# Routed experts without a token get no tile, and all expert weights are loaded ahead of the routed loop

## The chip, the cores and the metric

The kernel runs on one core of one Trainium2 chip. The metric is the device time of one execution in microseconds (us), with the inputs in HBM and the output written back to HBM. Shorter is better.

## The reference

Four sequences of 256 tokens of 256 float32 channels (1,024 tokens in all) pass a gated additive attention term and then a gated mixture of experts:

```python
si = einsum('bnd,d->bn', ctx, Wi[0]);  sj = einsum('bnd,d->bn', ctx, Wj[0])
xij = sigmoid(si[:, :, None] + sj[:, None, :] + b[0])
x = x + tanh(g_xattn[0]) * (0.6 * xij + 0.4 * layernorm(x))

xf = layernorm(x).reshape(-1, 256)                  # 1024 tokens
scores = sigmoid(xf @ w_router)                     # 32 experts
sfc = scores + corr_bias
grp = sfc.reshape(T, 8, 4)                          # 8 groups of 4
group_scores = top_k(grp, 2)[0].sum(-1)             # the best 4 groups stay
topk_idx = top_k(where(score_mask, sfc, -inf), 6)   # 6 experts a token
combine = zeros((T, 32)).at[...].add(take_along_axis(scores, topk_idx))
g = einsum('th,ehm->etm', xf, gate_w); u = einsum('th,ehm->etm', xf, up_w)   # M = 176
eo = einsum('etm,emh->eth', silu(g) * u, down_w)
routed = einsum('te,eth->th', combine, eo)
shared = silu(xf @ sh_gate_w) * (xf @ sh_up_w) @ sh_down_w                   # M = 352
x = x + tanh(g_ffn[0]) * (routed + shared)
```

There are 1,024 x 6 = 6,144 pairs of token and expert. How they fall on the experts depends on the inputs.

## The kernel before

The kernel is written engine by engine, with semaphores by hand. All is float32.

**Ahead of the routed loop.** The sequencer of SyncE (SP) starts the loads of the inputs, the shared weights and then the expert weights, four experts in four transfers (`load_expert_weights`, L215: gate, up, and two parts of down). Before the loop it does so for the first 20 of 32 transfers (`FIRST`, L56, L247), that is for the first 20 experts. In the meantime the engines work out the attention term, both layer norms, the router and the choice of experts, and after that the shared expert in 16 units.

**Sorting.** Every expert owns a region of 1,152 rows in a DRAM buffer, `rows_dram`. A row has 289 numbers (1,156 bytes): 256 channels, 32 combine weights and the token's number. GpSimd scatters the rows of the 1,024 tokens there, six copies each, in 48 indirect transfers of 128 rows (L365). Behind an expert's last row 128 pad rows are written, so that its last tile is full: for 20 experts by SP (L253 to L256), for 12 (`ACT_PADS`) by ScalarE's queue (L467 to L471). One more block of 128 pads, the idle one, stands behind all regions (L251). GpSimd's queue also clears two buffers for the sums (L359).

**The table of tiles.** VectorE turns the counts of rows into numbers of tiles of 128 rows each, at least one for every expert (L901 to L903), and from that makes a table with the expert and the first row of every tile. The numbers of rounds come from the total: `last` is one plus how many of 11, 15, 19, ... are below the total (L906 to L908, L336), and 4 x last + 7 tiles are run (`RING` is 4, `REST` is 3). Surplus tiles read the idle block.

**The routed loop.** For each tile SP loads 128 rows (L272; the first load waits for all pads and all scatters, L266 and L267). PE transposes x (L649), multiplies with gate and up (L578), transposes h (L584, L585) and multiplies with down (L593, L594). ScalarE copies, applies silu and scales; VectorE copies and gates; GpSimd adds the result to one of the two sums in DRAM by an indirect accumulating transfer (L384). Tiles run in rounds of four, with four buffers for the rows. In SP's first rounds (`LATE`, L57) a reload of each buffer is followed by one of the 12 late weight transfers (L284 to L287). The rounds after that stand in a loop with an If on `last` (L288). PE waits for the first 20 transfers before its first tile (L656) and for the other 12 after four rounds (L698). At the end SP loads the two sums, VectorE adds them and SP stores the output.

Of the kernel before, what the change touches and what calls it, by code (L numbers as in the profile page):

```python
# [18 lines left out]
ALU = mybir.AluOpType  # L19
ACT = mybir.ActivationFunctionType  # L20

P = 128
# [5 lines left out]
RING = 4  # L28
# [5 lines left out]
def gated_xattn_moe(nc, x, ctx, g_xattn, g_ffn, w_adj, b_adj, w_router, corr_bias, gate_w, up_w, down_w,  # L34
# [3 lines left out]
    E, _, M = gate_w.shape  # L38
# [7 lines left out]
    PAIRS = T * TOPK  # L46
    TILES = (PAIRS - E) // P + E
    FULL, REST = TILES // RING, TILES % RING
# [4 lines left out]

    PLACED = [range(0, GROUP), range(GROUP, 2 * GROUP), range(2 * GROUP, J)]
    SUMS = 2
    FIRST = E * 5 // 8  # L56
    LATE = 1 + (E - FIRST) // RING  # L57
    PAD_TURN = 7
    ACT_PADS = 12
    TABLE_TURN = 6  # L60
# [2 lines left out]
    with ExitStack() as stack:  # L63
# [6 lines left out]
        def sem(name):  # L70
            return stack.enter_context(nc.semaphore(name))
# [53 lines left out]
        cnt_i = sb("cnt_i", [P, 2, E], I32)  # L125
        ntile = sb("ntile", [P, E])
# [6 lines left out]
        tile_of = sb("tile_of", [P, 2])  # L133
        used = sb("used", [P, 1])
        tiles = sb("tiles", [2, P], I32)
        LEAST = -(-(E - REST) // RING) - 1
        round_ends = sb("round_ends", [1, FULL - 2])
        round_ends_i = sb("round_ends_i", [1, FULL - 2], I32)
        round_is = sb("round_is", [1, FULL - 2])
# [39 lines left out]

        s_xin = [sem(f"s_xin{b}") for b in range(B)]  # L180
        s_ctx, s_wadj, s_gates, s_cb, s_wr = (sem(n) for n in ("s_ctx", "s_wadj", "s_gates", "s_cb", "s_wr"))
        s_shw, s_expw = sem("s_shw"), [sem("s_expw0"), sem("s_expw1")]

        s_const, s_clear = sem("s_const"), sem("s_clear")

# [29 lines left out]
        def load_expert_weights(eng, n):  # L215

            e = n // 4 * 4
            if n % 4 < 2:  # L220
                w, cols = ((gate_w, slice(0, M)), (up_w, slice(M, 2 * M)))[n % 4]
                ins = eng.dma_start(wgu[:, e:e + 4, :, cols].rearrange("p e k m -> p (e k) m"),  # L222
                                    w[e:e + 4].rearrange("e (k p) m -> p (e k) m", p=P))
            elif n % 4 == 2:
                ins = eng.dma_start(wd0[:, e:e + 4, :], down_w[e:e + 4, 0:P, :].rearrange("e p c -> p e c"))  # L225
            else:
                ins = eng.dma_start(wd1[:, e:e + 4, :], down_w[e:e + 4, P:M, :].rearrange("e p c -> p e c"))  # L227
            ins.then_inc(s_expw[0 if e < FIRST else 1], 16)

        @block.sync  # L230
        def _(sp):
# [9 lines left out]
            for s in range(SH):  # L241
# [2 lines left out]
                sp.dma_start(sgu[:, s, :, M:2 * M], sh_up_w[:, cols].rearrange("(k p) m -> p k m", p=P)).then_inc(s_shw, 16)  # L244
                sp.dma_start(sd0[:, s, :], sh_down_w[s * M:s * M + P, :]).then_inc(s_shw, 16)
                sp.dma_start(sd1[:, s, :], sh_down_w[s * M + P:(s + 1) * M, :]).then_inc(s_shw, 16)
            for n in range(FIRST):  # L247
                load_expert_weights(sp, n)

            sp.wait_ge(s_const, 4)  # L250
# [23 lines left out]
            def reload(i, s):  # L274
                t = i * RING + s

                sp.wait_ge(s_xT, t - (RING - 1))
                sp.wait_ge(s_taken, t - (RING - 1))
                load(t, s)

            load(0, 0, first_row)
            for s in range(1, RING):
                load(s, s)
            for i in range(1, LATE):  # L284
                for s in range(RING):
                    reload(i, s)
                    load_expert_weights(sp, FIRST + (i - 1) * RING + s)  # L287
            with sp.Fori(LATE, FULL) as i:  # L288
                with sp.If(i < last + 1):
                    for s in range(RING):  # L290
                        reload(i, s)
# [226 lines left out]
        def _(pe):  # L518
# [3 lines left out]
            for j in range(J):  # L522
                ins = nc.tensor.transpose(pX[j // 4][0:D, (j % 4) * P:(j % 4 + 1) * P], ctx_sb[:, j, :], ident[:, :])
# [129 lines left out]
                pe.wait_ge(s_xTc, t + 1)  # L653
                gate_up(None, par, lambda k: xT[:, par, k, :], lambda k: wgu[:, bass.ds(e, 1), k, :])

            pe.wait_ge(s_expw[0], 16 * FIRST)  # L656

            def look_up(t):
                return pe.value_load(tiles[0:1, bass.ds(t, 1)], min_val=0, max_val=E - 1)
# [9 lines left out]
            def iteration(i, first=False, tiles=None):  # L669


                e = e_next = None
                for s in range(tiles or RING):
                    left = tiles - s if tiles else RING
                    t = i * RING + s
                    e_before, e = e, e_next
                    if left > 2:
                        transpose_x((s + 2) % RING, i + (s + 2) // RING + 1, s % 2)
                    if left > 1:
                        e_next = look_up(t + 1)  # L680
                        routed_gate_up(t + 1, (s + 1) % 2, e_next)

                    if s == 0 and not first:
                        e_before = look_up(t - 1)
                    if s == 1:
                        e_before = look_up(t - 1)
                    turn_h(t + UNITS, s % 2)
                    if e_before is not None:
                        routed_down(t - 1, (s + 1) % 2, e_before)
                return e  # L690

            early = (FIRST - 1) // RING
            iteration(0, first=True)
            with pe.Fori(1, early) as i:
                iteration(i)
            pe.wait_ge(s_expw[1], 16 * (E - FIRST))  # L698
            last = load_last(pe)
            with pe.Fori(early, FULL - 1) as i:  # L700
                with pe.If(i < last):
                    iteration(i)
            e_last = iteration(last, tiles=RING + REST)
# [5 lines left out]
        def _(dve):  # L709
# [3 lines left out]
            def link(ins):  # L713

                made[0] += 1
                ins.then_inc(s_dve, 1)
                dve.wait_ge(s_dve, made[0])
# [182 lines left out]

            link(V.tensor_scalar(cnt_i[:, 0, :], ntile[:, :], float(P - 1), None, ALU.add))  # L901
            link(V.tensor_scalar(cnt_i[:, 1, :], cnt_i[:, 0, :], P.bit_length() - 1, None, ALU.logical_shift_right))
            link(V.tensor_scalar(ntile[:, :], cnt_i[:, 1, :], 1.0, None, ALU.max))  # L903
            link(V.tensor_tensor_scan(tend[:, :], ntile[:, :], zero_e[:, :], 0.0, ALU.add, ALU.add))

            link(V.tensor_scalar(round_is[:, :], round_ends[:, :], tend[0:1, E - 1:E], None, ALU.is_lt))  # L906
# [97 lines left out]
```

## Time and profile before

| | us |
|---|---|
| median of 3 runs | 329.17 |
| lowest and highest | 328.31, 332.16 |
| span of the profiled execution | 334.7 |

| engine | busy us | share of the span |
|---|---|---|
| PE (matmul) | 274.3 | 82% |
| PE (weight load) | 160.8 | 48% |
| DVE | 126.2 | 38% |
| ACT | 99.2 | 30% |
| POOL | 166.9 | 50% |

The profile is one execution, recorded by the hardware profiler; its span is 5.5 us above the median of the runs that were only timed. Engines: PE is TensorE, DVE VectorE, ACT ScalarE, POOL GpSimd, SP SyncE; SPq is SP's sequencer, which issues transfers. Busy shares are means over stages with different limits. The DMA share is the mean busy share of the core's 16 DMA engines; where packets overlap it comes to a little over 1. In all, 57.20 MB are moved. L12 is line 12 of the kernel.

### The profile page before, as it was taken

To read this page: it belongs to the slowest core of one execution; us is meant where nothing else is said; L and a number is where in the kernel's file an instruction comes from. 1 tells how busy PE (TensorE), PEld (TensorE's weight loads), DVE (VectorE), ACT (ScalarE), POOL (GpSimd) and SP (SyncE) were. 2 spreads that over 40 slices of the span, in tenths; PEclk is the share of its full clock that TensorE was granted. 3 is DMA by queue.
4 is the path that set the end of the run, shared out by engine and by line. 5 is a ranking of instruction groups with operands and counts; after the bars stand their busy time and mean duration, and the time that the engine had idled before them with its cause. 6 is when DMAs were issued, how large, how long until landed. Compare 5 with 4: busy or idle time off the path is not lost.

```text
span 334.7 us, 6384 instructions
## 1 busy us (share of the span) xinstructions
PE 274.3 (82%) x1107; PEld 160.8 (48%) x1108; DVE 126.2 (38%) x627; ACT 99.2 (30%) x267; POOL 166.9 (50%) x145
## 2 busy tenths in 40 slices
PE   4673879999205997998999999999999999999700
PEld 3531445555002654655565655555566555665300
DVE  4568689433100331332333333333333333333214
ACT  3452411111001332333333333333333333333200
POOL 3334777777700153344555555555555555465620
PEclk9999999999655998999999999999999999999955
DMA  5899999999974589995666566666666666664577
GB/s 157 266 319 366 352 343 314 314 230 254 240 154 114 156 211 259 229 249 91 100 99 99 98 100 89 113 100 89 96 109 96 94 100 100 100 99 71 59 170 240
DMA packets 58557, 57.20 MB, mean 171 GB/s; under 512 B 6544, under 2 KB 56432, under 8 KB 58544
## 3 DMA queue, kind: packets, MB, share of 16 engines
q1 hardware_dynamic: 43520, 36.51, 39.6%
q0 software_dynamic: 13136, 18.78, 34.0%
q10 hardware_dynamic: 1888, 1.78, 2.5%
q8 instruction: 4, 0.07, 0.1%
q14 instruction: 9, 0.07, 0.1%
HBM read 32.35 MB, written 24.70 MB: 170 GB/s over the span
## 4 chain that ended last, share of the span: by engine, by line
PE 53%; SPq 24%; DMA 15%; issue 4%; DVE 1%; ACT 1%; DVEq 0%; POOLq 0%; ACTq 0%
PE pG L578 23%; PE pY L594 11%; PE pY L593 8%; PE pX L649 7%; DMA sum_dram<-xnT,idx 6%; SPq L225 5%; SPq L222 5%; DMA rows_dram<-pad_rows 4%; SPq L227 4%; SPq L255 4%; DMA rows<-rows_dram 3%; SPq L256 3%; PE pH L584 2%; PE pH L585 2%; DMA xnT<-sum_dram 1%
## 5 line engine op out<-in xcount | busy, mean ns | idle before, releaser
L384 POOL DMA_INDIRECT sum_dram<-xnT,idx x71 | 110.0, 1549 | 119.1 <-ACT xnT L486 94.9
L578 PE MATMUL pG<-wgu,rows 128*128 x284 | 99.9, 476 | 2.0 <-ACT rows L476 1.5
L855 DVE COPY hT<-pH 128x128 f32<-128x128 f32 x87 | 25.3, 291 | 119.7 <-PE pH L585 117.9
L578 PEld LDWEIGHTS pG<-wgu,rows 128*128 128x128 f32 x284 | 49.9, 196 | 19.8 <-issue 5.4
L365 POOL DMA_INDIRECT rows_dram<-rows,row_i x48 | 47.3, 986 | 21.3 <-issue 14.2
L486 ACT ACTIVATE xnT<-pY,wt 128x256 f32<-128x256 f32 x71 | 33.7, 474 | 73.9 <-PE pY L594 41.8
L462 ACT ACTIVATE sg<-pG 128x176 f32<-128x176 f32 x87 | 27.6, 317 | 90.9 <-PE pG L578 90.9
L594 PE MATMUL pY<-wd,hT 48*128 x142 | 49.4, 428 | 0.0
L649 PE MATMUL pX<-ident,rows 128*128 128x128 f32 x142 | 31.7, 306 | 21.0 <-DMA rows<-rows_dram 21.0
L593 PE MATMUL pY<-wd,hT 128*128 x142 | 42.6, 382 | 0.0
L649 PEld LDWEIGHTS pX<-ident,rows 128*128 128x128 f32 x142 | 14.8, 144 | 44.8 <-issue 40.1
L476 ACT ACTIVATE rows<-pX 128x256 f32<-128x256 f32 x71 | 26.9, 379 | 27.7 <-PE pX L649 25.4
L594 PEld LDWEIGHTS pY<-wd,hT 48*128 48x128 f32 x142 | 20.9, 184 | 23.5 <-issue 23.5
L851 DVE TENSOR_TENSOR h<-sg,pG 128x176 f32<-128x176 f32 x87 | 27.8, 319 | 4.9 <-ACT sg L462 4.9
L939 DVE COPY wt<-rows 128x1 f32 x71 | 10.9, 154 | 38.2 <-issue 20.4
L584 PE MATMUL pH<-ident,h 128*128 128x128 f32 x87 | 24.1, 277 | 0.9 <-DVE h L851 0.9
L585 PE MATMUL pH<-ident,h 128*48 128x128 f32 x87 | 23.9, 274 | 0.0
L856 DVE COPY hT<-pH 48x128 f32<-48x128 f32 x87 | 23.7, 273 | 0.0
L578 PE MATMUL pG<-sgu,xnT 128*128 128x352 f32 x64 | 22.9, 481 | 0.0
L593 PEld LDWEIGHTS pY<-wd,hT 128*128 128x128 f32 x142 | 21.6, 193 | 0.8 <-issue 0.3
L584 PEld LDWEIGHTS pH<-ident,h 128*128 128x128 f32 x87 | 12.3, 142 | 12.1 <-DVE h L851 2.9
L943 DVE COPY idx<-rows 128x1 int32<-128x1 int32 x71 | 10.6, 149 | 12.4 <-DMA sum_dram<-xnT,idx 12.2
(145 smaller groups left out, 168.7 us busy)
## 6 DMA issues: line engine op xcount, KB each, us to landing
rows<-rows_dram SPq DMA_DIRECT2D x71, 144.5 KB, 2.2
wgu<-in_L_ffn_gate_w_dram SPq DMA_DIRECT2D x8, 704.0 KB, 7.6
wgu<-in_L_ffn_up_w_dram SPq DMA_DIRECT2D x8, 704.0 KB, 9.1
wd<-in_L_ffn_down_w_dram SPq DMA_DIRECT2D x8, 512.0 KB, 8.4
rows_dram<-pad_rows SPq DMA_DIRECT2D x21, 144.5 KB, 12.7
sum_dram<-pad_rows POOLq DMA_DIRECT2D x2, 1152.0 KB, 10.9
rows_dram<-pad_rows ACTq DMA_DIRECT2D x12, 144.5 KB, 8.4
wd<-in_L_ffn_down_w_dram SPq DMA_DIRECT2D x8, 192.0 KB, 7.4
```

The source lines that it names most:

```text
L365: pool.indirect_dma_start(rows_dram[:, :], bass.IndirectOffsetOnAxis(ap=row_i[:, j, k:k + 1], axis=0), rows[:, j, :], None).then_inc(s_sca ...
L384: pool.indirect_dma_start(sums_dram[s % SUMS][:, :], bass.IndirectOffsetOnAxis(ap=idx[:, s:s + 1], axis=0), y[:, s, :], None, compute_op=A ...
L462: nc.scalar.activation(sg[:, par, :], pG[par][:, 0:M], ACT.Silu).then_inc(s_silu, 1)
L476: nc.scalar.activation(xT[:, par, :, :].rearrange("p k t -> p (k t)"), pX[par][:, 0:K * P], ACT.Copy).then_inc(s_xTc, 1)
L486: nc.scalar.activation(y[:, s, :], pY[s % 2][:, 0:H], ACT.Copy, scale=wt[:, s:s + 1]).then_inc(s_yc, 1)
L578: ins = nc.tensor.matmul(pG[par][:, 0:2 * M], left(k), w(k), start=(k == 0), stop=(k == K - 1))
L584: nc.tensor.transpose(pH[par][:, 0:P], h[:, par, 0:P], ident[:, :])
L585: nc.tensor.transpose(pH[par][0:M2, P:2 * P], h[:, par, P:M], ident[:, :]).then_inc(s_hT, 1)
L593: nc.tensor.matmul(bank[:, 0:H], hT[:, par, 0, :], w0, start=start, stop=False)
L594: ins = nc.tensor.matmul(bank[:, 0:H], hT[0:M2, par, 1, :], w1, start=False, stop=stop)
L649: ins = nc.tensor.transpose(pX[par][:, k * P:(k + 1) * P], xg[:, s, k * P:(k + 1) * P], ident[:, :])
L851: V.tensor_tensor(h[:, par, :], sg[:, par, :], pG[par][:, M:2 * M], ALU.mult).then_inc(s_h, 1)
```

## The change

Three things change. The number of tiles of an expert is no longer raised to one where it has no rows. All 32 weight transfers are issued by SP ahead of its pads, under one semaphore, and the loop's reloads stand in one loop with an If. PE waits for all weights before the first tile, and its rounds stand in one loop with an If from round 1 on. `LEAST`, a lower bound that is declared for the value of `last`, follows the new least number of tiles.

```diff
--- before.py
+++ after.py
@@ -53,8 +53,6 @@
 
     PLACED = [range(0, GROUP), range(GROUP, 2 * GROUP), range(2 * GROUP, J)]
     SUMS = 2
-    FIRST = E * 5 // 8
-    LATE = 1 + (E - FIRST) // RING
     PAD_TURN = 7
     ACT_PADS = 12
     TABLE_TURN = 6
@@ -133,7 +131,7 @@
         tile_of = sb("tile_of", [P, 2])
         used = sb("used", [P, 1])
         tiles = sb("tiles", [2, P], I32)
-        LEAST = -(-(E - REST) // RING) - 1
+        LEAST = -(-(PAIRS // P - REST) // RING) - 1
         round_ends = sb("round_ends", [1, FULL - 2])
         round_ends_i = sb("round_ends_i", [1, FULL - 2], I32)
         round_is = sb("round_is", [1, FULL - 2])
@@ -179,7 +177,7 @@
 
         s_xin = [sem(f"s_xin{b}") for b in range(B)]
         s_ctx, s_wadj, s_gates, s_cb, s_wr = (sem(n) for n in ("s_ctx", "s_wadj", "s_gates", "s_cb", "s_wr"))
-        s_shw, s_expw = sem("s_shw"), [sem("s_expw0"), sem("s_expw1")]
+        s_shw, s_expw = sem("s_shw"), sem("s_expw")
 
         s_const, s_clear = sem("s_const"), sem("s_clear")
 
@@ -225,7 +223,7 @@
                 ins = eng.dma_start(wd0[:, e:e + 4, :], down_w[e:e + 4, 0:P, :].rearrange("e p c -> p e c"))
             else:
                 ins = eng.dma_start(wd1[:, e:e + 4, :], down_w[e:e + 4, P:M, :].rearrange("e p c -> p e c"))
-            ins.then_inc(s_expw[0 if e < FIRST else 1], 16)
+            ins.then_inc(s_expw, 16)
 
         @block.sync
         def _(sp):
@@ -244,7 +242,7 @@
                 sp.dma_start(sgu[:, s, :, M:2 * M], sh_up_w[:, cols].rearrange("(k p) m -> p k m", p=P)).then_inc(s_shw, 16)
                 sp.dma_start(sd0[:, s, :], sh_down_w[s * M:s * M + P, :]).then_inc(s_shw, 16)
                 sp.dma_start(sd1[:, s, :], sh_down_w[s * M + P:(s + 1) * M, :]).then_inc(s_shw, 16)
-            for n in range(FIRST):
+            for n in range(E):
                 load_expert_weights(sp, n)
 
             sp.wait_ge(s_const, 4)
@@ -281,11 +279,7 @@
             load(0, 0, first_row)
             for s in range(1, RING):
                 load(s, s)
-            for i in range(1, LATE):
-                for s in range(RING):
-                    reload(i, s)
-                    load_expert_weights(sp, FIRST + (i - 1) * RING + s)
-            with sp.Fori(LATE, FULL) as i:
+            with sp.Fori(1, FULL) as i:
                 with sp.If(i < last + 1):
                     for s in range(RING):
                         reload(i, s)
@@ -653,7 +647,7 @@
                 pe.wait_ge(s_xTc, t + 1)
                 gate_up(None, par, lambda k: xT[:, par, k, :], lambda k: wgu[:, bass.ds(e, 1), k, :])
 
-            pe.wait_ge(s_expw[0], 16 * FIRST)
+            pe.wait_ge(s_expw, 16 * E)
 
             def look_up(t):
                 return pe.value_load(tiles[0:1, bass.ds(t, 1)], min_val=0, max_val=E - 1)
@@ -691,13 +685,9 @@
 
 
 
-            early = (FIRST - 1) // RING
             iteration(0, first=True)
-            with pe.Fori(1, early) as i:
-                iteration(i)
-            pe.wait_ge(s_expw[1], 16 * (E - FIRST))
             last = load_last(pe)
-            with pe.Fori(early, FULL - 1) as i:
+            with pe.Fori(1, FULL - 1) as i:
                 with pe.If(i < last):
                     iteration(i)
             e_last = iteration(last, tiles=RING + REST)
@@ -900,7 +890,7 @@
 
             link(V.tensor_scalar(cnt_i[:, 0, :], ntile[:, :], float(P - 1), None, ALU.add))
             link(V.tensor_scalar(cnt_i[:, 1, :], cnt_i[:, 0, :], P.bit_length() - 1, None, ALU.logical_shift_right))
-            link(V.tensor_scalar(ntile[:, :], cnt_i[:, 1, :], 1.0, None, ALU.max))
+            link(V.tensor_copy(ntile[:, :], cnt_i[:, 1, :]))
             link(V.tensor_tensor_scan(tend[:, :], ntile[:, :], zero_e[:, :], 0.0, ALU.add, ALU.add))
 
             link(V.tensor_scalar(round_is[:, :], round_ends[:, :], tend[0:1, E - 1:E], None, ALU.is_lt))
```

## Rows read from the trace of the kernel before

**Rows 1.** The page, PE and DMA in 40 slices of the span, tenths.
```profile
PE   4673879999205997998999999999999999999700
...
DMA  5899999999974589995666566666666666664577
```

**Rows 2.** Windows by stage: length, busy by engine, granted clock, DMA share, GB/s.
```profile
12.00:20.00 8.00, 4.41 (x13) 2.25 (x11) 5.54 (x18) 5.05 (x12) 2.40 (x3) 1.00 1.07 321
28.00:58.00 30.00, 23.40 (x99) 12.66 (x100) 24.14 (x141) 6.24 (x16) 22.82 (x24) 1.00 1.09 338
58.00:66.00 8.00, 7.72 (x31) 4.33 (x30) 3.87 (x18) 0.95 (x3) 6.17 (x7) 1.00 1.07 328
66.00:98.00 32.00, 19.45 (x73) 10.75 (x72) 7.40 (x28) 1.91 (x6) 19.77 (x21) 0.82 1.05 230
98.00:102.00 4.00, 0.00 (x0) 0.00 (x0) 0.00 (x0) 0.00 (x0) 0.00 (x0) 0.50 0.15 47
...
160.00:300.00 140.00, 140.00 (x594) 83.66 (x595) 47.92 (x249) 54.07 (x149) 76.52 (x50) 1.00 0.63 99
```

**Rows 3.** Timeline of SP's queue: start us, us, line, transfer, count.
```profile
11.14 0.43 SPq L222 DMA_DIRECT2D wgu<-in_L_ffn_gate_w_dram  x1
...
16.72 0.45 SPq L222 DMA_DIRECT2D wgu<-in_L_ffn_gate_w_dram  x1
...
58.24 0.47 SPq L251 DMA_DIRECT2D rows_dram<-pad_rows  x1
60.33 27.93 SPq L256 DMA_DIRECT2D rows_dram<-pad_rows  x20
101.38 4.88 SPq L272 DMA_DIRECT2D rows<-rows_dram  x5
```

**Rows 4.** Waits of SP's queue, 85 to 105 us: total, times, longest.
```profile
SPq L267 <- DMA rows_dram<-rows,row_i: 9.4, 1, 9.4
SPq L272 <- DMA rows_dram<-pad_rows: 1.8, 1, 1.8
```

**Rows 5.** Chain of waits, the piece before the first load: start us, us, what.
```profile
87.66 13.55 DMA rows_dram<-pad_rows
```

**Rows 6.** Timeline of POOL, the last of its 48 scatters.
```profile
90.90 0.96 POOL L365 DMA_INDIRECT rows_dram<-rows,row_i  x1 [0.30 <-issue]
```

**Rows 7.** Timeline of PE, first transpose of h of tiles 1, 13 and 68.
```profile
112.35 0.27 PE L584 MATMUL pH<-ident,h 128*128 128x128 f32 x1
...
153.44 0.27 PE L584 MATMUL pH<-ident,h 128*128 128x128 f32 x1
...
309.27 0.27 PE L584 MATMUL pH<-ident,h 128*128 128x128 f32 x1
```

**Rows 8.** The page's DMA issues: count, KB each, median us to landing.
```profile
rows<-rows_dram SPq DMA_DIRECT2D x71, 144.5 KB, 2.2
wgu<-in_L_ffn_gate_w_dram SPq DMA_DIRECT2D x8, 704.0 KB, 7.6
wgu<-in_L_ffn_up_w_dram SPq DMA_DIRECT2D x8, 704.0 KB, 9.1
wd<-in_L_ffn_down_w_dram SPq DMA_DIRECT2D x8, 512.0 KB, 8.4
rows_dram<-pad_rows SPq DMA_DIRECT2D x21, 144.5 KB, 12.7
...
wd<-in_L_ffn_down_w_dram SPq DMA_DIRECT2D x8, 192.0 KB, 7.4
```

**Rows 9.** DMA queue q1 (SP's), packets, MB, share: 66 to 98, 329.8 to 334.6 us.
```profile
q1 hardware_dynamic: 2382, 2.45, 36.8%
...
q1 hardware_dynamic: 1110, 1.07, 66.3%
```

## The prediction

> **What bounds the kernel now.** I read the 40 slices of the page first. The reader is to see two stages with different limits. In the first, up to about 98 us, the DMA row stands at 8 and 9 while PE comes and goes, and PE is empty just before the routed loop; in the second, PE stands at 9 until the last two slices and DMA at about 6 [rows 1]. The windows by stage put numbers on that: DMA share 1.05 to 1.09 in every stretch from 12 to 98 us, then 0.63 with PE busy 140.00 of 140 us [rows 2].
>
> Next come SyncE's own queue and the chain of waits. SP issues five groups of four experts' weights from 11.14 on. It spends 58.24 - 16.72 = 41.5 us on the last four, 10.4 us each. At 58.24 it reaches the pads: one, then twenty that take it 27.9 us, and the first routed load goes out at 101.38 [rows 3]. SP waits for the scatters 9.4 us and for pads 1.8 us before that load [rows 4], and the chain runs back through a pad of 13.55 us [rows 5]. So pads and scatters end together, and what ends them is the volume that 16 busy DMA engines must move. GpSimd issued its last scatter at 90.90 [rows 6]. The routed loop itself is bound by PE.
>
> PE's first transpose of h in each tile is a good clock for the loop. From 153.44 to 309.27 it ticks 55 times in 155.83 us, 2.833 us a tile. From 112.35 (tile 1) to 153.44 (tile 13) it needs 41.09 us where 12 tiles at that pace are 34.0, so 7.1 us are lost while the last twelve weight transfers run beside the loop. From 309.27 (tile 68) to the span's end are 25.4 us [rows 7].
>
> **Removed: tiles.** The kernel runs whole rounds of four tiles after the first seven, 4 x last + 7. Working out the reference's routing on its own inputs gives 7 of 32 experts without a token and 64 tiles by the rounded-up counts, 71 when each absent expert gets one. 71 needs last = 16, thus 71 tiles, which is the count of routed loads on the page [rows 8]. 64 lies over 63, so last = 15 and 67 tiles run: seven tiles go, but only one round. Four tiles by 2.833 are **11.3 us off PE's path**. Clearing or padding does not shrink: the pads still go out for all 32 experts. The replaced VectorE instruction works on the same 32 columns as before and I cost it at nothing: all of it is hidden, since the table is through long before 101 us. The If that now guards rounds 1 to 3 as well is the one that rounds 4 to 15 already carry at an unbroken 2.833, and the rounds skipped at the end (two before, three after) leave no gap at the tail that I can see; nothing for both. Were such a skip to cost as much as 0.5 us, it would show as a gap on PE.
>
> **Moved: three groups of weights.** Each is 704 + 704 + 512 + 192 KB [rows 8], 2.16 MB, together 6.49 MB in twelve transfers, from between the reloads to ahead of the pads on SP's queue. Queued behind them on SP are all 21 of its pads, and behind those the first routed load; PE, ScalarE, VectorE and GpSimd all wait for that load. PE's wait for all weights costs nothing of its own, as they stand ahead of the pads on the same queue.
> - Gain in the loop: SP and the DMA engines are free of weights there. The stage behind it (share 0.63) shows no loss, so I take back **7.1 us**, all of it.
> - Cost ahead of the loop, the disputed term d. I work it out by volume. From 58 to 98 us 2.63 + 7.36 = 10.0 MB move (328 GB/s for 8 us, 230 for 32) and 0.2 MB more in the next 4 [rows 2]. Of these 21 pads of 0.148 MB, 3.1 MB, are SP's. After the change weights, scatters and ScalarE's 12 pads run together: 10.2 - 3.1 + 6.5 = 13.6 MB. The row nearest to that mix is 58 to 66 us, all three kinds at once, at 328 GB/s: 41.4 us, to 99.6. Then SP's 3.1 MB of pads run last. The nearest row for pads is 66 to 98 us at 230 GB/s: 13.5 us, to 113.1. The engines used to fall idle at 98, so **d = 15 us**, and the first load goes out at 101.4 + 15 = 116.4.
> - Bounds of d. Low: the mix at the 338 GB/s of 28 to 58 us [rows 2] is 40.2 us, and lone pads as fast as the stores of the output, 1.07 MB in 66.3% of 4.8 us or 336 GB/s [rows 9], are 9.2 us; end 107.6, d = 9.6. High by volume: the weights simply added at the 321 GB/s that SP's queue made alone from 12 to 20 us [rows 2] are 20.2 us. Higher still is the second rival. I keep 230 for the pads since it is the only row with these 1156-byte rows written.
>
> The Trainium skill, page "DMA: Bandwidth & Descriptors", section "Measured", gives 425 GB/s for one core streaming a large transfer. The three groups would then be an estimated 15.3 us in place of 20.2 when simply added. The traces here show 321 to 338 over any stretch with weights, so I keep the rows.
>
> **The sum.** Tile 1 turns at 112.35 + 15 = 127.35; tile 64, the third last of 67, 63 ticks later at 305.8; 25.4 us on, the span ends at 331.3. Or: 334.7 - 11.3 - 7.1 + 15 = 331.3 us, 3.4 us less. The profiled execution stands at 334.7 where the median of the runs is 329.17; I carry the difference of 3.4 over and predict **325.8 us**, 1.0% less. The break-even is d = 18.4. A measurement of this kernel can tell about 2%, 6.6 us, from no change; that is d below 11.8 or above 25.
>
> **The rivals.**
> - *Likeliest, within 2%* (d from 11.8 to 25), chance 0.65. The gains and the delay nearly cancel, whichever of the two volume counts holds.
> - *Faster by over 2%*, chance 0.24. Two things could bring it. Pads left alone could drain at the 336 GB/s of a lone store queue [rows 9], with reads of weights mixed well with writes of scatters (338 beside scatters against 321 alone, [rows 2]): d = 9.6, end 334.7 - 18.4 + 9.6 = 325.9, median 320.4. Against it: 230 GB/s from 66 to 98 us was all writes of short rows, and dropping ScalarE's and GpSimd's share does not make those rows longer.
> - *Slower by over 2%: the pads keep their pace.* Chance 0.11. SP comes to the pads three groups of 10.4 later, at 89.4, and they then take what they took before: from the first of the twenty at 60.33 to the last one's landing at 101.2 [rows 3, 5], 40.9 us. They start 2.1 later, so 91.5 + 40.9 = 132.4, d = 31, end 347.3, median 341.8. For it: nothing in the trace shows SP's pads by themselves. Against it: they were slow while scatters and ScalarE's pads took their turns, with SP's queue holding 36.8% of the engines' time from 66 to 98 us [rows 9]; GpSimd's scatters end at 90.90 and do not wait for SP. It decides from d = 25, which is pads at 3.1 MB in 23.5 us, 132 GB/s.
>
> The Trainium skill, page "DMA: Bandwidth & Descriptors", section "Queues, rings and completion order", says that each DMA engine takes turns among the queues that have work. By that rule a lone pad queue gets the whole engine, which speaks against this rival; no run here shows it yet.
> - *The tile count doesn't fall as counted.* Chance under 0.02, within the 0.11. If the kernel's own rounding left 68 or more tiles, all 71 would run: 342.6, median 337.1. Expert counts close to a multiple of 128 (639 to 640, 139 to 128) are not near enough to add four.
>
> **How the numbers follow.** The faster case holds 0.24, no change 0.65, slower 0.11. The range that leaves no more than 2 in 10 out takes d from 9.6 less a microsecond, 319.5, to d of about 23, 334; within the likeliest alone it is 322.5 to 335.7.
>
> **What would show it.** SP's first pad at 89 to 97 us. DMA share at or over 1 without a break from 12 to about 110 us, with more than 320 GB/s up to some 99 and 200 to 340 after. The first routed load at 116 (111 to 122); 131 refutes the volume count and shows the slow rival. PE's tiles 2.83 apart from the second on, 67 of them, so that the loop from first load to last tile loses no 7 us. The tail from the third last tile unchanged at 25.4. Wrong would be: a gap on PE in the loop's first rounds (then something other than weights made it), 71 or 63 loads, or pads that land long after the engines' share has fallen below 1.

## The result

The changed kernel takes 342.62 us (median of 4, 342.49 to 343.85), the kernel before 329.18 us. The ratio is 1.0385, with a 95% interval from 1.0331 to 1.0438: slower by 3.9%, where 1.0% faster was forecast. The range ended at 334.0. A later set of runs on another chip gave 1.0382 (1.0302 to 1.0463).

The profiled execution of the changed kernel spans 340.8 us, 6.1 more than the 334.7 of the profile before. That is less than half of the 13.4 us between the medians. The time of an execution is its span plus 1.6 to 2.0 us in every kernel measured since. If that held for the profile before as well, its execution took some 336.5 us, 7 above the median; that time itself is not known.

Page of the changed kernel, PE, granted clock, DMA and GB/s in 40 slices (to set beside [rows 1]):

```profile
PE   3673889999200008999999999999999999999800
...
PEclk9999999999855555999999999999999999999965
DMA  5999999999983332366656665665655656664478
GB/s 154 285 313 355 344 348 353 353 304 314 310 278 107 104 104 69 70 102 98 101 97 98 101 98 96 99 100 93 103 99 98 101 97 97 98 101 72 50 146 268
```

Windows by stage of the same kernel (length, busy by engine, granted clock, DMA share, GB/s; to set beside [rows 2]):

```profile
66.00:98.00 32.00, 21.15 (x80) 11.76 (x79) 7.64 (x29) 2.22 (x7) 19.71 (x21) 0.88 1.08 318
98.00:108.00 10.00, 0.00 (x0) 0.00 (x0) 0.00 (x0) 0.00 (x0) 0.00 (x0) 0.50 0.47 153
...
112.00:116.00 4.00, 0.00 (x0) 0.00 (x0) 0.00 (x0) 0.00 (x0) 0.00 (x0) 0.50 0.32 105
...
120.00:124.00 4.00, 0.00 (x0) 0.00 (x0) 0.00 (x0) 0.00 (x0) 0.00 (x0) 0.50 0.33 110
```

The stage that the forecast did not have stands in the slices: between the busy DMA stage and the loop there are 28 us in which every compute engine is idle while the DMA engines fall to a share of a third, 105 to 117 GB/s in the windows from 108 to 124 us. Bandwidth is not what is short there. Timeline of SP's queue (start us, us, line, transfer, count; to set beside [rows 3]):

```profile
95.00 1.30 SPq L225 DMA_DIRECT2D wd<-in_L_ffn_down_w_dram  x1
96.34 0.44 SPq L249 DMA_DIRECT2D rows_dram<-pad_rows  x1
98.10 26.11 SPq L254 DMA_DIRECT2D rows_dram<-pad_rows  x20
125.94 184.41 SPq L270 DMA_DIRECT2D rows<-rows_dram  x67
```

The last of the weights is issued at 95.00, the twenty pads take SP 26.1 us, and the first load follows at 125.94. Ahead of that load SP's queue waited for pads once, for 0.2 us, and not for scatters (before: 9.4 and 1.8 us for scatters and pads, [rows 4]):

```profile
SPq L270 <- DMA rows_dram<-pad_rows: 0.2, 1, 0.2
```

The chain of waits of the changed kernel shows what one pad is made of (start us, us, what):

```profile
120.67 0.27 SPq L253
121.37 0.33 SPq L254
121.85 0.27 SPq L253
122.67 0.34 SPq L254
123.17 0.27 SPq L253
123.87 1.90 DMA rows_dram<-pad_rows
125.94 0.36 SPq L270
```

L253 is the look-up of the pad's address in a table (0.27 us, up to 0.57 at the start of a group of four) and L254 the issue (0.34 us). With the register arithmetic, the check of the value and the loop's own steps between them, the twenty take 26.11 us, 1.31 us each. The chain goes through SP's instructions and not through transfers; only the last landing, 1.90 us, is on it. In the chain of the kernel before the last pad's landing was 13.55 us [rows 5].

Stage by stage, from PE's first transpose of h of each tile (changed kernel, tiles 1 and 64, the third last of 67):

```profile
136.79 0.27 PE L578 MATMUL pH<-ident,h 128*128 128x128 f32 x1
...
316.01 0.27 PE L578 MATMUL pH<-ident,h 128*128 128x128 f32 x1
```

| stage, us | before, profile of the forecast | changed | difference |
|---|---|---|---|
| up to the first routed load | 101.38 | 125.94 | +24.6 |
| first load to tile 1 | 10.97 | 10.85 | -0.1 |
| tile 1 to the third last tile | 196.92 | 179.22 | -17.7 |
| third last tile to the end | 25.43 | 24.79 | -0.6 |
| span | 334.7 | 340.8 | +6.1 |

### The profile page after: what moved, and what is told of

Read it like the earlier page. It is cut to its first block, busy times and chain, and to the rows that moved or that the text cites. A ratio compares the mean times of both kernels' runs of the same rounds, so it can differ in the third digit from the quotient of the medians.

```text
span 340.8 us, 6147 instructions
## 1 busy us (share of the span) xinstructions
PE 261.6 (77%) x1059; PEld 153.8 (45%) x1060; DVE 122.2 (36%) x607; ACT 94.6 (28%) x255; POOL 160.5 (47%) x141
## 3 DMA queue, kind: packets, MB, share of 16 engines
q1 hardware_dynamic: 42944, 35.92, 36.6%
## 4 chain that ended last, share of the span: by engine, by line
PE 55%; SPq 34%; issue 4%; DMA 4%; DVE 1%; POOL 0%; ACT 0%; DVEq 0%; POOLq 0%
PE pG L572 24%; PE pY L588 12%; SPq L223 11%; SPq L220 11%; PE pY L587 8%; PE pX L643 7%; SPq L225 3%; SPq L253 3%; SPq L254 2%; PE pH L579 2%; PE pH L578 2%; DMA xnT<-sum_dram 1%; DMA sum_dram<-xnT,idx 1%; DVE xs L962 1%; DMA rows<-rows_dram 1%
## 5 line engine op out<-in xcount | busy, mean ns | idle before, releaser
L378 POOL DMA_INDIRECT sum_dram<-xnT,idx x67 | 103.8, 1549 | 132.0 <-ACT xnT L480 127.2
L572 PE MATMUL pG<-wgu,rows 128*128 x268 | 92.8, 469 | 0.8 <-issue 0.8
L643 PE MATMUL pX<-ident,rows 128*128 128x128 f32 x134 | 30.0, 306 | 41.4 <-DMA rows<-rows_dram 41.4
L572 PEld LDWEIGHTS pG<-wgu,rows 128*128 128x128 f32 x268 | 46.7, 195 | 16.5 <-issue 2.7
L480 ACT ACTIVATE xnT<-pY,wt 128x256 f32<-128x256 f32 x67 | 31.8, 474 | 69.6 <-PE pY L588 39.7
L588 PE MATMUL pY<-wd,hT 48*128 x134 | 46.6, 428 | 0.0
L587 PE MATMUL pY<-wd,hT 128*128 x134 | 40.1, 381 | 0.0
L470 ACT ACTIVATE rows<-pX 128x256 f32<-128x256 f32 x67 | 25.4, 379 | 49.0 <-PE pX L643 46.0
L929 DVE COPY wt<-rows 128x1 f32 x67 | 10.3, 154 | 59.7 <-DMA rows<-rows_dram 40.6
L572 PE MATMUL pG<-sgu,xnT 128*128 128x352 f32 x64 | 24.3, 504 | 0.0
L587 PEld LDWEIGHTS pY<-wd,hT 128*128 128x128 f32 x134 | 20.2, 191 | 0.7 <-issue 0.3
L578 PEld LDWEIGHTS pH<-ident,h 128*128 128x128 f32 x83 | 11.7, 141 | 11.3 <-DVE h L841 2.9
L572 PEld LDWEIGHTS pG<-sgu,xnT 128*128 128x128 f32 x64 | 11.4, 199 | 7.4 <-issue 4.1
```

The source lines that it names most:

```text
L378: pool.indirect_dma_start(sums_dram[s % SUMS][:, :], bass.IndirectOffsetOnAxis(ap=idx[:, s:s + 1], axis=0), y[:, s, :], None, compute_op=A ...
L480: nc.scalar.activation(y[:, s, :], pY[s % 2][:, 0:H], ACT.Copy, scale=wt[:, s:s + 1]).then_inc(s_yc, 1)
L572: ins = nc.tensor.matmul(pG[par][:, 0:2 * M], left(k), w(k), start=(k == 0), stop=(k == K - 1))
L578: nc.tensor.transpose(pH[par][:, 0:P], h[:, par, 0:P], ident[:, :])
L587: nc.tensor.matmul(bank[:, 0:H], hT[:, par, 0, :], w0, start=start, stop=False)
L588: ins = nc.tensor.matmul(bank[:, 0:H], hT[0:M2, par, 1, :], w1, start=False, stop=stop)
```

## The experiments

Twelve kernels were run in three sets of four, each set on one chip with the kernel before beside it: 329.6 us on the first, 334.87 on the second, 329.9 on the third. Times of different sets are therefore compared by their ratio to the kernel before. Single places of two traces (SP's arrival at the pads, the first load) differ by 3 to 4 us between executions with the same instructions ahead of them, and by more between chips.

### Set 1: the parts of the change, and the pads on another queue

**The kernel before, profiled once more** (no edit).

> The kernel before, profiled once more. The profiled execution on which the prediction rests spans 334.7 us, 5.5 above the median of its runs, while the changed kernel's spans lie 1.7 us below its times. If the first profile caught a long execution, this one spans about 327.5 us, and the 7 us are missing at one place: either the loop's first 13 tiles run at 2.83 us each (no loss beside the late weights), or the first routed load goes out some 7 us before 101.4. If the two ways of timing only differ, the span is 334 to 335 again.

Measured: 329.86 us, 0.9988 of before (0.9943 to 1.0033). The profiled execution spans 329.6. SP's queue, its waits for the scatters and the pads, and the first transposes of h of tiles 1, 13 and 68:

```profile
60.43 26.80 SPq L256 DMA_DIRECT2D rows_dram<-pad_rows  x20
98.67 4.87 SPq L272 DMA_DIRECT2D rows<-rows_dram  x5
```

```profile
SPq L267 <- DMA rows_dram<-rows,row_i: 8.8, 1, 8.8
...
SPq L272 <- DMA rows_dram<-pad_rows: 0.7, 1, 0.7
```

```profile
109.57 0.27 PE L584 MATMUL pH<-ident,h 128*128 128x128 f32 x1
...
149.63 0.27 PE L584 MATMUL pH<-ident,h 128*128 128x128 f32 x1
...
305.46 0.27 PE L584 MATMUL pH<-ident,h 128*128 128x128 f32 x1
```

Neither of the two places alone holds the difference to the first profile. The first load goes out 2.7 us earlier, the loop's first tiles still lose 6.1 us (149.63 - 109.57 = 40.06 for 12 tiles of 2.833), and the tail is 1.3 us shorter. The loss beside the late weights is real. The execution profiled here took 331.44 us, 1.6 above the median, so this profile too is of a longer execution than most, but less so than the first. It is the better one to set the changed kernel against: first load 27.3 us later, tile 1 to third last tile 16.7 us shorter, tail 0.7 longer. Together that is 11.2 us of span.

**The tile part alone.**

```diff
-            link(V.tensor_scalar(ntile[:, :], cnt_i[:, 1, :], 1.0, None, ALU.max))
+            link(V.tensor_copy(ntile[:, :], cnt_i[:, 1, :]))
```

The declared bound `LEAST` follows, as in the change.

> The kernel before with the tile part of the change alone (the 12 late weight transfers stay in the loop; with these inputs no tile of the first four rounds belongs to an expert past the 20th). Both theories: one round of four tiles less at 2.833 us, so 11.3 us less than before, 317.9 us. If the end of the loop were bound by something other than PE, less than that.

Measured: 319.67 us, 0.9719 (0.9631 to 0.9807), 9.9 us less than before. 67 tiles ran, as counted. The tile part does what it says. The first load stands at 97.68 us, where before_again has 98.67.

**The weight part alone** (the same line, and `LEAST`, put back into the changed kernel).

> The changed kernel with at least one tile per expert again: 71 tiles. Weights ahead alone: 11.3 us above the changed kernel, 353.9 us, 24.7 above before. A first load at 126 as in the changed kernel.

Measured: 349.72 us, 1.0634 (1.0532 to 1.0736), so 20.1 us above before. That is 4 us less than expected; 2.7 of them are in the first load, at 123.19 us here and 125.94 in the changed kernel. The pads took SP the same (26.17 us), but it came to them at 93.28 instead of 96.34, with the same instructions ahead of them; so much differs from one execution to the next. The loss is all in the weight part, and the tile part hides half of it.

**All pads of experts on ScalarE's queue.**

```diff
-    ACT_PADS = 12
+    ACT_PADS = 32
...
-            with sp.Fori(0, (E - ACT_PADS) // 4) as q:
-                for i in range(4):
-                    at = sp.value_load(pad_at[0:1, bass.ds(q * 4 + i, 1)], min_val=0, max_val=IDLE - P)
-                    sp.dma_start(rows_dram[bass.ds(at, P), :], pad_rows[:, :]).then_inc(s_pads, 16)
...
-                for e in range(first, min(first + 2, E)) if n >= PAD_TURN else ():
+                for e in range(first, min(first + 2, E) if n < UNITS - 1 else E) if n >= PAD_TURN else ():
```

> The changed kernel with all 32 experts' pads issued by ScalarE's queue (two in each unit of the shared expert from the eighth on, the other 14 after the last unit), none by SP. Theory A, SP's own pace: the twenty pads cost SP 1.35 us each behind the weights, one after another, while the DMA engines stand at a third; then SP is free at 96 us and the first load goes out when the engines have moved all: 13.6 + 3.1 MB from 58 us on at 330 GB/s, 109 to 112 us, time 326 to 330 us. Theory B, pads are slow at the DMA engines when they are alone or last (107 GB/s measured): ScalarE's last 14 pads, 2.1 MB, come as late as 82 us and drain at 107 GB/s, while weights of SP take their turns; first load not before 118 us, time 334 us or more.

Measured: 330.43 us, 1.0021 (0.9982 to 1.0060), 12 us less than the changed kernel with the same bytes and the same tiles. Windows by stage of this kernel, and its SP queue:

```profile
66.00:98.00 32.00, 21.62 (x82) 11.99 (x80) 8.10 (x30) 2.22 (x7) 20.13 (x21) 0.90 1.10 295
98.00:110.00 12.00, 0.00 (x0) 0.00 (x0) 0.00 (x0) 0.00 (x0) 0.00 (x0) 0.50 1.09 306
110.00:115.00 5.00, 0.00 (x0) 0.00 (x0) 0.00 (x0) 0.00 (x0) 0.00 (x0) 0.50 0.53 146
```

```profile
108.75 0.44 SPq L249 DMA_DIRECT2D rows_dram<-pad_rows  x1
115.15 183.41 SPq L265 DMA_DIRECT2D rows<-rows_dram  x67
```

The first load goes out at 115.15, between the marks of the two theories, but nothing drains at 107 GB/s: the engines stay at a share of 1.09 or more up to 110 us and move 306 GB/s from 98 us on, where the changed kernel has them at 0.47 and then at a third. The hole in the DMA row is gone, and the time is that of the kernel before. The first load is 3 us later than theory A had it, as the mix ran at 295 to 306 GB/s and not at 330.

### Set 2: what a pad costs

**Each pad of SP's twice.**

```diff
         rows_dram = nc.dram_tensor("rows_dram", [IDLE + P, ROW], F32, kind="Internal").ap()
+        other_dram = nc.dram_tensor("other_dram", [IDLE + P, ROW], F32, kind="Internal").ap()
...
                     sp.dma_start(rows_dram[bass.ds(at, P), :], pad_rows[:, :]).then_inc(s_pads, 16)
+                    sp.dma_start(other_dram[bass.ds(at, P), :], pad_rows[:, :]).then_inc(s_pads, 16)
...
-            sp.wait_ge(s_pads, 16 * (E + 1))
+            sp.wait_ge(s_pads, 16 * (E + 1 + E - ACT_PADS))
```

> The changed kernel with a second transfer behind each of SP's twenty pads: same source, same register for the address, into another DRAM buffer that nobody reads; the first load waits for these too. It doubles the volume of the pads without a second look-up of the address. Theory A, the pace is that of SP's instructions (look-up, register arithmetic, issue): the extra issue is 0.34 to 0.45 us, so 7 to 9 us more, 350 to 352 us, and the DMA engines move 170 GB/s in that stretch instead of 107. Theory B, such writes drain at 107 GB/s when alone: the double volume takes 27 us more, 370 us.

Measured: 359.5 us, 1.0734 (1.0634 to 1.0833). By the ratio that is 353.3 us on the first chip, beside the 350 to 352 of theory A and the 370 of theory B. SP's queue, the idle block's pad, the first and the last pair, and the first load:

```profile
101.59 0.44 SPq L250 DMA_DIRECT2D rows_dram<-pad_rows  x1
...
103.53 0.39 SPq L255 DMA_DIRECT2D rows_dram<-pad_rows  x1
104.02 0.38 SPq L256 DMA_DIRECT2D other_dram<-pad_rows  x1
...
139.35 0.33 SPq L255 DMA_DIRECT2D rows_dram<-pad_rows  x1
139.78 0.38 SPq L256 DMA_DIRECT2D other_dram<-pad_rows  x1
142.43 184.82 SPq L272 DMA_DIRECT2D rows<-rows_dram  x67
```

Twenty pairs take 36.6 us (103.53 to 140.16), where twenty single pads took 26.1: 0.53 us for an extra transfer of 0.148 MB, not 1.31. The stage from 104 to 142 us moved 163 GB/s. Theory B, a drain at 107 GB/s, would have put the pairs at 55 us; it is refuted. Theory A holds, with the extra issue a little dearer (10.5 us in the stage) than the 7 to 9 expected.

**Eight more pads to ScalarE** (`ACT_PADS` 20, `PAD_TURN` 6; no other line).

> The changed kernel with 20 pads on ScalarE's queue (from its seventh unit on) and 12 on SP's. Theory A, SP's pace: eight pads of 1.35 us less for SP, 10.8 us, less what its weights lose because ScalarE's pads now take turns with them (SP came to its pad 12 us later when ScalarE had all 32): first load 117 to 121 us against 125.9, time 334 to 338 us. Theory B, the volume alone decides: no gain, 342 us.

Measured: 342.0 us beside 334.87 for the kernel before, 1.0251 (1.0176 to 1.0327). By the ratio that is 1.3% below the changed kernel, about 4.4 us, with intervals that hardly part (the changed kernel's begins at 1.0331). It is short of the 5 to 9 us that theory A's 334 to 338 us stand for. The time alone does not rule out theory B, which had no gain. SP's queue says more:

```profile
105.07 0.44 SPq L249 DMA_DIRECT2D rows_dram<-pad_rows  x1
107.10 15.27 SPq L254 DMA_DIRECT2D rows_dram<-pad_rows  x12
124.36 184.71 SPq L270 DMA_DIRECT2D rows<-rows_dram  x67
```

Twelve pads take 15.3 us, 1.27 each: SP saves 10.8 us on pads. But it comes to them at 105.07 instead of 96.34. Only part of that belongs to the edit. The kernel with doubled pads ran on this chip with the changed kernel's instructions up to the pads, and SP came to its first pad at 101.59 there. So some 5 us are the chip and the execution, and 3.5 us are left for weights that now share the engines with eight more pads (one trace of each). The first load, 124.36, missed the 117 to 121 expected, which were worked out on the first chip's trace. That moving a producer off SP pays only as far as the engines have room fits this, but is not shown by it.

**The tile part, made safe for all inputs.** With absent experts dropped, a tile of the first four rounds could need a late weight. With fewer than 17 tiles for the first 20 experts, each of those gets at least one again, by a test at run time:

```diff
+    EARLY = (FIRST - 1) // RING * RING + 1
...
-            link(V.tensor_scalar(ntile[:, :], cnt_i[:, 1, :], 1.0, None, ALU.max))
+            link(V.tensor_copy(ntile[:, :], cnt_i[:, 1, :]))
+            link(V.tensor_tensor_scan(tend[:, :], ntile[:, :], zero_e[:, :], 0.0, ALU.add, ALU.add))
+            link(V.tensor_scalar(used[:, :], tend[:, FIRST - 1:FIRST], float(EARLY), None, ALU.is_lt))
+            link(V.tensor_scalar(ntile[:, 0:FIRST], ntile[:, 0:FIRST], used[:, 0:1], None, ALU.max))
             link(V.tensor_tensor_scan(tend[:, :], ntile[:, :], zero_e[:, :], 0.0, ALU.add, ALU.add))
```

> The tile part alone, made safe for all inputs: absent experts get a tile only where the first 20 experts have fewer than 17 tiles between them, so that the four rounds ahead of PE's second wait never need a late weight (three more small VectorE instructions, about 0.1 us each, off the path). As the tile part alone: 319.7 us; if the table of tiles were on the path after all, up to 1 us more.

Measured: 326.2 us beside 334.87, 0.9783 (0.9711 to 0.9856). Within the intervals it is the tile part alone (0.9719). The absolute time is higher since this chip is slower for all. By the ratio it beats both the kernel before and the changed one.

**The same with the late weights on ScalarE's queue.**

```diff
             for i in range(1, LATE):
                 for s in range(RING):
                     reload(i, s)
-                    load_expert_weights(sp, FIRST + (i - 1) * RING + s)
...
             for i in range(2):
                 for s in range(RING):
                     turn(i, s, before=i)
+                    k = i * RING + s
+                    for n in range(FIRST + (E - FIRST) * k // (2 * RING), FIRST + (E - FIRST) * (k + 1) // (2 * RING)):
+                        load_expert_weights(act, n)
```

> As the last one, with the 12 late weight transfers issued from ScalarE's queue in the first eight tiles instead of from SP's behind each reload. If the 6 us that the loop loses in its first 13 tiles come from row loads that stand behind a weight transfer on the same queue, rows now take turns with weights and most of it comes back: 314 to 316 us. If they come from the load on the DMA engines as such (6.5 MB in a shorter time, with the accumulating transfers), it stays or grows: 319 to 323 us.

Measured: 325.0 us, 0.9751 (0.9680 to 0.9823): no different. The first transpose of h of tile 1 is at 109.84 and of tile 13 at 151.96, 42.1 us, 8.1 lost, against 6.4 in the kernel above (151.92 - 111.53 = 40.4). From 110 to 130 us the DMA share is 0.99 to 1.16, against 0.43 to 1.02 in the kernel above. So the loss in the loop does not come from rows that stand behind weights on one queue. The load on the engines is what is left of the two causes, and a higher share goes with a larger loss here; it was not shown by an experiment of its own.

### Set 3: order and instructions with the bytes unchanged

**The changed kernel again.**

> The changed kernel once more, on the chip of the next three runs, so that they stand beside it: 1.04 of the kernel before, SP's twenty pads at 1.31 us each with the engines at a third, and a first load some 27 us later than in the kernel before.

Measured: 342.95 us, 1.0382 (1.0302 to 1.0463). The profile repeats the first: pads from 98.77, 26.10 us, first load at 126.74.

**SP's pads written out.**

```diff
-            with sp.Fori(0, (E - ACT_PADS) // 4) as q:
-                for i in range(4):
-                    at = sp.value_load(pad_at[0:1, bass.ds(q * 4 + i, 1)], min_val=0, max_val=IDLE - P)
-                    sp.dma_start(rows_dram[bass.ds(at, P), :], pad_rows[:, :]).then_inc(s_pads, 16)
+            for e in range(E - ACT_PADS):
+                at = sp.value_load(pad_at[0:1, e:e + 1], min_val=0, max_val=IDLE - P)
+                sp.dma_start(rows_dram[bass.ds(at, P), :], pad_rows[:, :]).then_inc(s_pads, 16)
```

> The changed kernel with SP's twenty pads written out instead of in a loop of four, so that the look-up of each address needs no register arithmetic. Nothing else differs, no byte more or less. Theory A, SP's instructions set the pace behind the weights: ScalarE, which has its pads written out, issues one each 1.04 us when it does nothing else, so 20 x (1.31 - 1.04) = 5.4 us less than the changed kernel. Theory B, the writes themselves do: no difference.

Measured: 337.15 us, 1.0238 (1.0156 to 1.0320), 5.8 us less than the changed kernel on the same chip. SP's queue:

```profile
94.08 0.44 SPq L249 DMA_DIRECT2D rows_dram<-pad_rows  x1
95.53 21.56 SPq L253 DMA_DIRECT2D rows_dram<-pad_rows  x20
118.90 184.80 SPq L269 DMA_DIRECT2D rows<-rows_dram  x67
```

1.08 us a pad for 1.31, 4.5 us less for twenty, with every byte the same. Another 3.0 us of the earlier first load are SP's arrival at the pads (94.08 for 97.11). The edit stands behind that point, so these 3.0 us are the difference between executions seen above and not its doing. A few address instructions on SP take 4.5 us off the path to the first load; that could not be so where transfers set the pace.

**Pads ahead of the last twelve weight transfers.**

```diff
-            for n in range(E):
+            for n in range(20):
                 load_expert_weights(sp, n)
...
                     sp.dma_start(rows_dram[bass.ds(at, P), :], pad_rows[:, :]).then_inc(s_pads, 16)
+            for n in range(20, E):
+                load_expert_weights(sp, n)
```

> The changed kernel with SP's pads moved back to where they were, behind the first 20 weight transfers; the other 12 follow the pads and still stand ahead of the first routed load. Same bytes, same instructions, another order. Theory A: the pads' 27 us of SP's time lie beside the scatters again, and what is left is the volume. The 12 weights are issued from 87 us on and land by 112 to 119 us, PE starts then: 8 to 14 us less than the changed kernel, 329 to 335 us. Theory C, order is no matter because the engines' volume decides in either: as the changed kernel.

Measured: 333.48 us, 1.0104 (1.0030 to 1.0177), 9.5 us less than the changed kernel. SP's queue:

```profile
57.17 24.46 SPq L254 DMA_DIRECT2D rows_dram<-pad_rows  x20
...
115.64 186.00 SPq L272 DMA_DIRECT2D rows<-rows_dram  x67
```

The pads lie beside the scatters again. The first load goes out at 115.64, half a microsecond from the 115.15 of the kernel with all pads on ScalarE. The two are not at the same point, though. Here the last weights are still on their way (the last one is issued at 113.20, and from 115 to 116 us the DMA share is 1.06), and the first rows land in 5.1 us behind them. PE's first transpose of h of tile 1 comes 3.1 us later than in the kernel with all pads on ScalarE, and the whole kernel by as much (333.48 and 330.43 us). That kernel first, then this one:

```profile
125.00 0.27 PE L573 MATMUL pH<-ident,h 128*128 128x128 f32 x1
...
128.11 0.27 PE L580 MATMUL pH<-ident,h 128*128 128x128 f32 x1
```

**The kernel before with its pads written out** (the same edit as two above).

> The kernel before with the same twenty pads written out. Theory A: there the pads' issue is hidden, as 13 us of backlog stand behind the last of them; SP saves 5 us and waits 5 us longer for scatters and pads: no difference, within 1%. If SP's pace were the limit in the kernel before as well, 5 us less.

Measured: 330.2 us, 1.0006 (0.9968 to 1.0043). The pads take 24.75 us there, and SP waits 11.7 us for scatters and 1.3 for pads where it waited 8.8 and 0.7; the first load stands at 98.87. What SP saves it waits. In the kernel before, the pads' issue is free. The same twenty instructions took 21.56 us behind the weights and take 24.75 here, beside scatters: the load on the engines does lengthen them, by 3.2 us.

## Why the prediction was wrong

**The step that failed is the term d,** and in it two sentences: "Then SP's 3.1 MB of pads run last. The nearest row for pads is 66 to 98 us at 230 GB/s: 13.5 us". They price the pads by the bytes that they move; what set their pace were SP's own instructions. The mix ended where it was put: the forecast had the mix through at 99.6 us, SP's first pad at 89 to 97, and the trace has a DMA share of 1.08 up to 98 and 0.47 behind it, and the pad at 96.34. From there the twenty pads took 26.1 us of SP's own instructions, not 13.5 us of transfers. With the first look-ups and the last landing, the first load came 26 us after the mix, at 125.94 and not 116.4. That is outside the forecast's 111 to 122 and short of the 131 that was to show its rival; the sign that did come is the last one named for being wrong, pads that land long after the engines' share has fallen below 1.

**The price stood in the rows.** [rows 3] has the twenty pads at 27.9 us in the kernel before. I read that as SP being held up by full queues, as it is on its weights. The single issues, one level below that row, say otherwise. Pieces of the chain of waits of the kernel before:

```profile
68.02 0.33 SPq L256
68.50 0.48 SPq L255
...
69.40 0.33 SPq L256
...
85.27 1.56 SPq L256
```

Of the 19 issues of these pads that the chain shows, 16 took 0.33 to 0.38 us, at a share of over 1, just as in the hole of the changed kernel. Three took longer, 0.76, 0.54 and 1.56, together 1.9 us more than the others would: only so much can be a full queue that held SP, and without it the 27.9 are close to the 26.1 of the changed kernel. With that loop the twenty take 24.5 to 27.9 us in the six traces where scatters run beside them (before 27.93, pads ahead of the last weights 24.46) and 26.1 to 26.2 in the three where nothing does. So the load moved the total by 2 us at most in either direction, and the bulk of it was SP's own in both places. The text did cost the pads' pace, as the rival for slower, but for the wrong reason (other queues taking turns) and at a chance of 0.11. Its time, 341.8, lies close to the 342.6 that came, but by luck. It let the pads take 40.9 us from the first issue to the last landing, where they took 27.7 (98.10 to 125.8), with d = 31 and a span of 347.3 where 340.8 was measured; the carrying over to the median, 7 us too low, brought it back. It was to decide from d = 25; d was 24.6 against the profile of the forecast and 27.3 against the other one. The rule of the Trainium skill weighed there (page "DMA: Bandwidth & Descriptors", section "Queues, rings and completion order": an engine takes turns among queues with work) is not at odds with the traces; it says nothing of a queue that its issuer does not fill.

**d falls into two parts, shown separately.** The first load, against before_again's 98.67, is at 115.15 with all pads on ScalarE and at 115.64 with the pads ahead of the weights: 16.5 to 17 us later. Tile 1 in these two, against 109.57, is 15.4 and 18.5 us later. That is the volume, where the count gave 15 (9.6 to 20.2 as bounds). Up to the 125.94 and 136.79 of the changed kernel are 10.3 to 10.8 us more by the first load and 8.7 to 11.8 by tile 1, for SP's pads behind the weights. (These are single traces, so each difference is good to some 3 us.) Had the order been such that only the volume counted, the time would have been in the forecast's range, in the class "within 2%": those two kernels take 1.002 and 1.010 of before, if not the 0.99 of the forecast.

**The tiles.** 67 were run, as worked out, and one round less is 11.3 us. That skipped rounds leave no gap was off: every kernel with 67 tiles shows one tile interval of 3.5 to 3.6 us instead of 2.83 where PE leaves the loop with three skipped rounds (301.12 to 304.68 in the changed kernel), none of those with 71 tiles and two skipped rounds. PE's wait there is named issue, 0.46 us. That the third skipped round makes the gap is inferred from this; no run varied it alone. In the changed kernel:

```profile
301.12 0.27 PE L578 MATMUL pH<-ident,h 128*128 128x128 f32 x1
...
304.68 0.27 PE L578 MATMUL pH<-ident,h 128*128 128x128 f32 x1
```

So the tile part is worth 10.6 us, and 9.9 was measured.

**The loop's loss.** 7.1 us were taken back; in the changed kernel tiles follow each other at 2.83 from tile 1 on, and the loop is shorter by 17.7 us, of 18.4 forecast less the 0.7 above. Right. But the first profile shows the loss at its largest: with the late weights behind SP's reloads it is 6.1 in the second profile of before and 5.2 to 6.4 in the three other kernels that have them there.

**The sum against the median.** The sum was made on the span, 334.7, and the difference carried over to the median, 329.17, although the two stood 5.5 us apart. That hid that the profile was, by all signs, of a long execution. All executions since have a time 1.6 to 2.0 us above their span, so a span of 334.7 goes with some 336.5 us. With d = 24.6 put in, the sum gives a span of 340.9, where 340.8 was measured; that shows that the other terms hold between these two profiles. Carried over as it was, it would have given 335.3 for the median, 7.3 us short. With the 9.6 us in d this second error makes up the whole miss, from 325.8 to 342.6. What makes the kernel before vary was not settled: from its lowest to its highest time are 1.2 to 2.1% on one chip (4 to 19 executions), in the changed kernel 0.4 and 0.7% (4 each), with all pads on ScalarE 0.5% (10). Between its two profiles the first load differs by 2.7 us, the loss in the loop by 1.0, the tail by 1.3. The first two are stages in which the DMA engines are full. In the changed kernel SP's instructions end the first of them, and twenty pads in a loop behind the weights vary little (26.10 to 26.17 us in three traces), though SP's arrival at them does (93.28 to 97.11). A reason is not shown.

## What to carry to other kernels

Before you put work behind other work on an in-order queue, price it twice: by the bytes it moves and by the instructions its issuer needs, address look-ups and register arithmetic included; here the larger one counted once nothing else was running. To tell a busy issuer from a full queue, read the single issues and not the total of twenty: an issue that takes 0.33 us with the engines full is not held up, and one of 1.56 us may be. And prefetching into a stage that is already full of transfers moves its end by the volume, while the later stage gives back only what it lost before: here 15 to 18 us were paid for 5 to 7 returned.

## What the runs showed of the hardware

- A transfer with an address from a table costs SP 1.31 us inside a loop that works out the table's index (changed kernel, nothing beside it) and 1.08 us with the index written out; with scatters beside it 1.22 to 1.40 and 1.24. A second transfer with the same address register costs 0.53 us more.
- The busy share does not tell what the engines could still move. From 66 to 98 us it is 1.05 with scatters and pads at 230 GB/s [rows 2] and 1.08 with weights, scatters and pads together at 318.
- The ten kernels in which PE skips three rounds of a loop with an If show one tile interval 0.7 to 0.8 us longer at that place; the four in which it skips two show none.
